# A two-layer graph network on one core: the next round's first sums moved between the types of the third and of the fourth slot

## The reference

```python
h = relu(relu(layernorm(x)) @ node_proj_w.T + node_proj_b)
for l in range(2):
    trans = einsum('nh,tdh->tnd', h, edge_W[l])        # 8 types
    agg = segment_sum(trans[edge_type, src], dst)
    h = relu(gru_cell(agg, h, gru_wih[l], gru_whh[l], gru_bih[l], gru_bhh[l]))
out = x + h @ out_w.T + out_b
```

## Time and profile before

| what | us |
|---|---|
| median of 3 runs | 2007.2 (2001.24 to 2015.2) |
| the profiled execution | 2021.61 |
| its span, first to last instruction | 2019.8 |
| PE busy | 1548.0 (77% of the span) |
| POOL busy | 1194.0 (59%) |
| DVE busy | 806.9 (40%) |
| ACT busy | 499.7 (25%) |

### The profile page before, as it was taken

One profiled execution on the slowest core, in us unless ns is written; L12 is line 12 of the kernel. 1 busy time (PEld: TensorE's weight loads), 2 busy tenths in 40 slices (PEclk: granted clock), 3 DMA queues, 4 the chain that ended last, 5 costly groups with the idle time before them and its releaser, 6 DMA issues.

```text
span 2019.8 us, 32542 instructions
## 1 busy us (share of the span) xinstructions
PE 1548.0 (77%) x10440; PEld 1066.8 (53%) x10441; DVE 806.9 (40%) x3362; ACT 499.7 (25%) x959; POOL 1194.0 (59%) x1277
## 2 busy tenths in 40 slices
PE   6477888787878866877883888878787786687877
PEld 3244555454555544655662555545545454565665
DVE  6656262523433244454442223212433224444444
ACT  5233151513324112222220101110423411121222
POOL 6555666565666666666625666565565666666661
PEclk9688899998999978898885998899898997888889
DMA  8323728264462422222213866674334255222221
GB/s 196 110 63 103 238 84 270 59 218 128 148 205 64 137 73 79 78 79 77 77 36 105 273 226 225 219 254 129 85 105 117 77 140 116 73 73 72 70 75 30
DMA packets 183275, 251.81 MB, mean 125 GB/s; under 512 B 24322, under 2 KB 156580, under 8 KB 183140
## 3 DMA queue, kind: packets, MB, share of 16 engines
q0 software_dynamic: 58176, 119.22, 21.7%
q1 hardware_dynamic: 118644, 128.45, 20.3%
q10 hardware_dynamic: 6320, 2.41, 0.5%
HBM read 211.87 MB, written 38.12 MB: 124 GB/s over the span
## 4 chain that ended last, share of the span: by engine, by line
PE 35%; another core or an unknown queue 31%; issue 11%; DVE 11%; DMA 4%; ACT 3%; DVEq 3%; SPq 2%; ACTq 0%; PEldq 0%
PE ps L1185 10%; PE ps L1257 5%; PE ps L1122 5%; PE ps L1162 4%; PE ps L1236 4%; DMA blocks<-node_table 4%; PE ps L1249 3%; PE ps L1228 2%; DVE acc L1850 1%; DVE onehot L1772 1%; DVE acc L1870 1%; ACT counts L871 1%; DVE onehot L1807 1%; DVE work L1728 1%
## 5 line engine op out<-in xcount | busy, mean ns | idle before, releaser
L660 POOL DMA_INDIRECT gath<-node_table,srcT x1212 | 1159.5, 957 | 774.7 <-issue 303.2
L1185 PE MATMUL ps<-counts,blocks 128*128 128x504 f16 (+3 forms) x1764 | 421.1, 386 | 66.8 <-issue 33.4
L1870 DVE TENSOR_TENSOR acc<-ps,acc 128x16 f32 x864 | 150.7, 174 | 792.4 <-remote 311.8
L950 ACT COPY sums_sb<-ps 128x512 f32<-128x512 f32 x216 | 126.3, 587 | 870.3 <-remote 600.3
L1185 PEld LDWEIGHTS ps<-counts,blocks 128*128 128x128 bf16 x1764 | 171.5, 101 | 266.1 <-issue 81.2
L1162 PE MATMUL ps<-work 128*128 128x392 bf16 x983 | 219.3, 358 | 119.5 <-ACT counts L871 43.2
L1257 PE MATMUL ps<-sums_sb,wT 128*128 128x128 f32 x1728 | 243.6, 299 | 59.9 <-ACT sums_sb L950 46.6
L1257 PEld LDWEIGHTS ps<-sums_sb,wT 128*128 128x128 f32 x1728 | 230.6, 212 | 74.6 <-ACT sums_sb L950 51.4
L1249 PE MATMUL ps<-onehot,gath 128*128 128x128 bf16 x2592 | 200.5, 230 | 62.6 <-issue 36.2
L1249 PEld LDWEIGHTS ps<-onehot,gath 128*128 128x128 bf16 x2592 | 177.8, 104 | 108.9 <-issue 74.9
L871 ACT CAST counts<-ps 128x392 f16<-128x392 f32 x429 | 188.3, 498 | 117.8 <-PE ps L1162 70.2
(11 more groups left out here) (209 smaller groups left out, 831.6 us busy)
## 6 DMA issues: line engine op xcount, KB each, us to landing
blocks<-node_table SPq DMA_DIRECT2D x84, 672.0 KB
kept_counts<-counts SPq DMA_DIRECT2D x28, 882.0 KB
counts<-kept_counts SPq DMA_DIRECT2D x28, 882.0 KB
gath<-node_table,srcT POOLq DMA_INDIRECT x1212
node_table<-gath SPq DMA_DIRECT2D x12, 360.0 KB, 4.5
node_table<-work SPq DMA_DIRECT2D x12, 360.0 KB
counts<-in_x_dram SPq DMA_DIRECT2D x1, 2880.0 KB
out_dram<-counts SPq DMA_DIRECT2D x12, 240.0 KB
```

What stands on the lines that cost most here:

```text
L660: nc.gpsimd.indirect_dma_start(out=gath[:, b, j, :], out_offset=None, in_=tables[l], in_offset=bass.IndirectOffsetOnAxis(ap=index, axis=0) ...
L950: act.copy(n_sb[:, b // 2, b % 2 * BG:(b % 2 + 1) * BG, :], narrow_sums[b % 2]) \
L1185: last = nc.tensor.matmul(head_ps[:, 0:COLS[share]], blocks[:, j % 2, at, part * H:(part + 1) * H], counts[:, a, 0:COLS[share]], start=(i ...
L1870: nc.vector.tensor_tensor(win, narrow_ps[q][:, g * NARROW:(g + 1) * NARROW], win, ALU.add) \
```

## The change

In a wide round PE no longer begins with the sums of slot 0. It runs the sums of slot 0 of the round that follows between the types of slots 2 and 3. The sums of slot 0 of round 38 stand ahead of the loop, and the last round begins without them, as round 47 has run them. The lists of places get a fifth entry for this. The same is done in the passes of the fallback (`later_places`), which these inputs don't enter. No other engine's program changes.

```diff
                 def first_places(phase, turns=0):
-                    places = [(phase + b) % PLACES for b in range(SLOTS)]
+                    places = [(phase + b) % PLACES for b in range(SLOTS + 1)]
                     return [(turns + ((phase + b) // PLACES + 1) * (16 * BG), place) for b, place in enumerate(places)]
 
                 def later_places(n):
-                    return [(n * (16 * BG) + 16 * BG, b) for b in range(SLOTS)]
+                    return [((n + b // SLOTS) * (16 * BG) + 16 * BG, b % SLOTS) for b in range(SLOTS + 1)]
 
                 def one_round(k, n, places):
                     begin, tile = round_tile(pe, mybir.EngineType.PE, n)
-                    sum_by_code(k, places[0][0], 0, places[0][1])
                     sum_by_code(k, places[1][0], 1, places[1][1])
                     piece(pe, begin, gates_begin, k, tile)
                     by_type(k, 0)
...
                     piece(pe, begin, gate_z, l + 1, tile)
                     sum_by_code(k, places[3][0], 3, places[3][1])
                     by_type(k, 2)
+                    sum_by_code(k + SLOTS, places[SLOTS][0], 0, places[SLOTS][1])
                     by_type(k, 3)
                     piece(pe, begin, to_rows, l + 1, tile)
...
                 def last_round(k, places, begin=None):
-                    sum_by_code(k, places[0][0], 0, places[0][1])
                     if begin is not None:
                         piece(pe, begin, gates_mid, k, l + 1)
...
                 begun = NARROW_END * SLOTS - HEAD_BATCHES[l]
+                landed, place = first_places(begun)[0]
+                sum_by_code(NARROW_END * SLOTS, landed, 0, place)
                 with pe.Fori(0, turns) as t:
...
+                        sum_by_code(p * BATCHES, 16 * BG, 0, 0)
                         with pe.Fori(0, ROUNDS - 1) as n:
```

## The result

The kernel before took 2011.2 us (median of 4 runs, 2001.2 to 2016.8), the changed kernel 2048.9 us (4 runs, 2040.9 to 2053.6). The ratio is 1.017, with a 95% interval of 1.0121 to 1.0219. By the medians the change costs 38 us, where I had forecast 4; the time lies 20 us above the top of my range. The profiled execution took 2045.0 us around a span of 2043.2. In the profile after, DVE's lines stand two further down: L1633 is L1631 of before, L1627 is L1625, L1589 is L1587, L1852 is L1850.

A forecast was written before the change was run, and what follows sets the result against it. No single engine was the bound; wide rounds went by PE's order and its two stops for DVE. Costs of 2.6 + 1.6 = +4.2 us, gains 0, on a 2007.2 us median gave 2011 us, range 1990 to 2029.

The forecast's parts named there:

- When the rows are seen: Between rounds: consumers see the rows only about when PE's whole block ends, which does not move; cost per round 0.
- 0.2 us a seam: Where one round's rows stand directly ahead of the next round's gates: 13 x 0.2 = 2.6 us lost.
- H: Theory formed after the result, not forecast: PE's completions are held back while GpSimd streams gathers and come out when it pauses.
- A gather of a later slot is let go earlier; nothing waits on POOL, so 0.: GpSimd's gathers in wide rounds: released earlier by up to the types and rows, but counted as no gain, 0 us.
- list of gains: Possible savings in PE's waits, register loads, ACT's copy and earlier gathers; each was taken as 0 us.
- rows 5 and 6: Profile excerpts at round ends in second and first layer: consumers start 2.06 and 2.48 us after the rows end.
- (A): Rows between rounds are seen at once, so every such place pays: +15 to +27 us, 2022 to 2034; chance 0.16.
- (B): Fewer matmuls queued behind the rows bring their completion forward at round ends: 1992 us; chance 0.10.
- (C): Gathers set the pace of the wide rounds after all, so earlier release shortens them: -28 us, 1979 us; chance 0.04.
- The last rounds: End of each pass: without sums between rows and gates only waiting is left, 2 x 0.8 = 1.6 us lost.

The follow-up runs named there:

- held kernel: Changed kernel, but GpSimd's third gather batch of a wide round also waits for the next sums; 2050.6 us, 1.0042 of the kernel before on a late chip.
- execution of 2022 us: Profiled execution of the unaltered changed kernel, rerun on another late chip; shortest of its ten, 2022.1 us, while that run's median was 2045.9 us, ratio 1.0127.
- run with the last rounds undone: Changed kernel, but each layer's last round keeps its own first sums at its start; 2035.5 us, 1.0069 of the kernel before on a late chip.

## Why the prediction was wrong

**The step that failed is "When the rows are seen".** I saw that DVE and ACT get the rows 2 us late, beside the end of PE's two sums, and took the end of PE's block for the cause; as that end doesn't move, I charged 0.2 us a seam. The row was right and the reading was not. In the earlier trace rows two things end near 1823.4, PE's block and a pause of GpSimd that began at 1822.51, and I looked only at PE. The change let GpSimd go on through that pause, and a round of the second layer costs 2.5 us more, where the sum had 0.2: the stop grows from 0.9 to 6.7 us, the first two gate matmuls behind the stop shown above take 1.96 us at a granted clock of 0.50 instead of 1.07 us at 1.00, and the z gate's stop of 3.5 us goes. The held kernel shows that the gathers make the delay of the rows: it alters one wait of GpSimd alone and takes the 7.6 us to 0.8. The kernels with half of the gathers show that PE's order by itself costs nothing that these runs can tell. How much of the 38 us the delay of the rows makes is not shown: the held kernel, on another chip, still has rounds of 26.8 us. And H is not the whole rule, as the first layer of the trace of after shows.

**"A gather of a later slot is let go earlier; nothing waits on POOL, so 0."** This is where the cost sat, in the list of gains. I had priced the gathers as transfers that somebody might wait for. What they did here was to occupy the stretch in which PE's completions should have come through. The 31% in the earlier trace rows whose releaser the profile could not name went with this effect (1% with half of the gathers, none on the prompt chip), and I read past them: a share of that size was to be explained before anything was costed at nothing.

**The rule of the Trainium skill** ("TensorE: Matmul & The Clock Gate", "What overlaps and what doesn't") says that matmuls start and end strictly in order. By that rule the 12 or 24 matmuls behind the rows could not be the reason for the delay, and I set the rule aside because the rows were seen late. On prompt chips the rows are seen 0.01 us after their end with 12 matmuls behind them and with 24, which fits the rule; on late ones the recorded ends are in order too, and it is the sight of them that is late. So my sentence that the trace does not agree in rows 5 and 6 was wrong: the two agree once end and sight are kept apart.

**Rivals.** (A), rows seen at once, +15 to +27 us, had the size nearest to the result and the wrong mechanism: where rows are seen at once the change costs 6 us, and where it costs 29 to 38 they are seen later than before in the second layer. (B), a shorter tail brings the completion forward, is excluded in the second layer of after: half the tail, four times the delay. In the first layer of that trace the delays did fall, from 0.4 to 2.5 us to 0.0 to 1.9; in the execution of 2022 us they are 0.0 to 8.3 there, so nothing can be built on it. (C), the gathers set the pace, is false for its reason and right for its suspect on late chips; on prompt chips it is plainly so, and the times don't gain by it, since nothing in the change makes GpSimd's stream shorter.

**The last rounds.** I had 0.8 us each. The gates of the last rounds stand idle as follows, in the first and the second pass after, and then in the second pass before; the first answers to the 1.95 us of the earlier trace rows:

```profile
1046.79 0.66 PE L1122 MATMUL ps<-hT,wT 128*128 128x250 f32 x2 [2.51 <-DVE work L1627]
...
2019.86 0.45 PE L1122 MATMUL ps<-hT,wT 128*128 128x250 f32 x1 [1.50 <-DVE counts L1633]
```

```profile
1996.31 0.66 PE L1122 MATMUL ps<-hT,wT 128*128 128x250 f32 x2 [0.94 <-DVE counts L1631]
```

2.51 - 1.95 and 1.50 - 0.94 are both +0.56 us, 1.1 us where I had 1.6, so this term was of the right size. The run with the last rounds undone asks for more, 0.6 to 1.0% between its ratio and those of the whole change, but these intervals are wide, its executions spread over 30 us, and they compare different chips. From the first sums of round 46 to the last sums of the pass the traces of after and of that run take 65.0 and 62.4 us in the second pass, 66.4 and 64.8 in the first, 4.2 us in all; whether the ends cost more than that stays open.

**The first layer.** The trace of after has it 3.9 us shorter in the wide rounds, the trace of 2022 us no shorter than before (262.3 against 261.4 us). The kernel that changes this layer alone never met a late chip, so how the 29 to 38 us divide between the layers there is known from single traces only. Why the rows of the first layer are seen soon although GpSimd streams is open.

None of the kernels tried beats the kernel before on either kind of chip; those with half of the gathers leave part of the computation out.

## What to carry to other kernels

When a consumer starts long after its producer's recorded end, and several completions come out together, ask what *else* ended at that moment, on every engine, GpSimd's gathers among them; two things that end together are two candidates, and a cause is not chosen by which of them the change leaves alone. A large share of a chain with no nameable releaser is a term of the sum, not background. And where an edit frees a buffer earlier, follow what is started with it, even if nobody waits for the result. And before a change without a record of its own is called late, look whether its consumer had already started.

## What the runs showed of the hardware that I had not expected

Chips differ by more than this change does. The kernel before took 2011 us in the first group of runs and 2017 to 2039 us on three other late chips, but 1622 to 1628 us on four prompt ones, with equal busy times of POOL (1194.0 and 1192.2 us in the two traces), DVE and ACT. In the late trace 391 of the 1016 completions of PE that have a record are seen over 0.5 us late, but only 2 of ACT's and 8 of DVE's; in the prompt one none of PE's and ACT's and one of DVE's, although GpSimd streams its gathers there without a pause. On a late chip half of the gathers left 28 late completions of PE and took a quarter of the time away. So the effect goes with the gathers, but these alone do not make it, and what makes a chip late is open. The mean granted clock is 0.886 in the late trace of before and 0.955 in the prompt one; PE waits more in the late one, and I read the clock as a consequence, which no run tested.

A late kernel can lock into a pattern that repeats round after round (after: 27.2 to 28.2 us, rows 7.5 to 7.8 us late) or miss it in another execution of the same program on another late chip (22.2 to 25.1 us, rows up to 4.3 us late, and 7.8 once, ahead of round 46). There its times spread over 36 us, and those of the kernel before over 29.
